# A two-layer pair-attention kernel: in layer 0, both attends of a period are put beside scores, and queries and keys are projected row by row

## What is computed

```python
x = group_norm(x); x = (x - mu) * rsqrt(var + EPS) * ln_w + ln_b
q, k, v = proj(wq), proj(wk), proj(wv)
g = sigmoid(proj(wg_w) + wg_b)
bias = einsum('hc,bcij->bhij', wb, x)
scores = einsum('bhcij,bhcik->bhijk', q, k) * scale + bias[:, :, None, :, :]
a = softmax(scores, axis=-1)
o = g * einsum('bhijk,bhcik->bhcij', a, v)
x = x + einsum('oc,bcij->boij', wrep_w, o) + wrep_b
```

## Time and profile before

| | |
|---|---|
| median of 3 runs | 4764.48 us (4764.19 to 4767.61) |
| the profiled execution | 4769.83 us |
| its span, first to last instruction | 4768.0 us |
| TensorE busy with matmuls | 4524.0 us (95%) |
| DVE, ACT, POOL busy | 3883.6, 3755.4, 3632.2 us |
| layer 0, first to last `residual` | 492.2 to 2785.2 us |

### The profile page before, as it was taken

The page is one execution under the profiler, slowest core; times in us unless marked ns, Lnnn a source line. Parts: engine busy times, 40 slices in busy tenths (PEclk is TensorE's granted clock), DMA queues, the critical chain, the costliest instruction groups (busy, mean ns, idle before and its releaser), DMA issues. The chain is left out here.

```text
span 4768.0 us, 152284 instructions
## 1 busy us (share of the span) xinstructions
PE 4524.0 (95%) x43063; PEld 3665.8 (77%) x43063; DVE 3883.6 (81%) x12844; ACT 3755.4 (79%) x11408; POOL 3632.2 (76%) x6054
## 2 busy tenths in 40 slices
PE   5556999999999999999999979999999999999998
PEld 1224777777777777777777768888888998888887
DVE  5443888889888888888888968888888888888887
ACT  2335888888888888888888868888888888888886
POOL 3442888888888889888888837777777777777776
PEclk7778999999999999999999989999999999999999
DMA  9996111111111111111111111111111111111111
GB/s 359 353 352 196 55 63 53 62 62 53 62 53 62 53 62 58 56 61 54 62 53 62 54 36 55 53 53 53 53 53 53 49 50 53 53 53 53 53 53 35
DMA packets 237444, 383.57 MB, mean 80 GB/s; under 512 B 18756, under 2 KB 156616, under 8 KB 224968
## 3 DMA queue, kind: packets, MB, share of 16 engines
q1 hardware_dynamic: 237256, 381.63, 23.7%
HBM read 309.21 MB, written 72.35 MB: 80 GB/s over the span
## 5 line engine op out<-in xcount | busy, mean ns | idle before, releaser
L1758 POOL TENSOR_SCALAR l_probs<-l_probs,l_inv 128x256 f32<-128x256 f32 x2048 | 947.8, 482 | 374.0 <-DVE l_inv L1655 374.0
L713 POOL TENSOR_SCALAR l_probs<-l_probs,l_inv 128x256 f32<-128x256 f32 x2048 | 944.0, 482 | 118.4 <-DVE l_inv L1140 117.9
L1040 ACT ACTIVATE l_probs<-l_probs,l_neg_max 128x256 f32<-128x256 f32 x2048 | 1019.3, 501 | 12.0 <-DVE l_neg_max L1132 4.4
L1556 ACT ACTIVATE l_probs<-bank,l_neg_max 128x256 f32<-128x256 f32 x2048 | 944.8, 477 | 46.0 <-DVE l_neg_max L1649 39.2
L1662 DVE TENSOR_TENSOR l_probs_t<-bank,bias 128x512 f32<-128x512 f32 x1024 | 669.8, 686 | 130.5 <-PE bank L1468 116.2
L1132 DVE CUSTOM_DVE_ANT_0 l_probs<-bank,bias 128x256 f32<-128x256 f32 x2048 | 744.0, 420 | 25.2 <-issue 12.9
L1649 DVE TENSOR_REDUCE l_neg_max<-bank 128x2 f32<-128x512 f32 x1024 | 675.2, 682 | 43.0 <-PE bank L1456 33.9
L931 PE MATMUL bank<-ident,l_probs 128*128 128x128 f32 x4096 | 615.1, 278 | 0.3 <-ACT l_probs_t L1079 0.3
L931 PEld LDWEIGHTS bank<-ident,l_probs 128*128 128x128 f32 x4096 | 467.9, 141 | 137.6 <-issue 44.3
L1468 PE MATMUL bank<-ident,l_probs 128*128 128x128 f32 x4096 | 559.9, 274 | 5.3 <-POOL l_probs L1758 3.9
L969 PE MATMUL bank<-l_probs_t,l_v 128*64 128x256 f32 x4096 | 498.5, 385 | 0.7 <-ACT l_probs_t L1079 0.7
(11 more groups left out here) (205 smaller groups left out, 13617.6 us busy)
## 6 DMA issues: line engine op xcount, KB each, us to landing
fp_x<-in_x_dram SPq DMA_DIRECT2D x32, 1024.0 KB, 6.2
fp_ln_w<-in_L_conv_ln_w_dram SPq DMA_DIRECT2D x32, 1024.0 KB, 8.3
fp_ln_b<-in_L_conv_ln_b_dram SPq DMA_DIRECT2D x32, 1024.0 KB, 10.8
fp_pair<-in_L_conv_pair_repr_dram SPq DMA_DIRECT2D x32, 1024.0 KB, 10.8
l_x<-in_x_dram SPq DMA_DIRECT2D x128, 256.0 KB, 2.9
l_ln_w<-in_L_conv_ln_w_dram SPq DMA_DIRECT2D x128, 256.0 KB, 3.2
l_ln_b<-in_L_conv_ln_b_dram SPq DMA_DIRECT2D x128, 256.0 KB, 3.5
x<-l_y SPq DMA_DIRECT2D x128, 256.0 KB, 2.0
```

The costliest lines, as they stand in the source:

```text
L713: last = nc.gpsimd.tensor_scalar(probs[:, r, h, c], probs[:, r, h, c], inv[:, r, h, c:c + 1], 1.0, ALU.mult, ALU.mult)
L1040: last = nc.scalar.activation(probs[:, r, h, c], probs[:, r, h, c], ACT.Exp, bias=neg_max[:, r, h, c:c + 1], scale=-1.0, accum_out=total[: ...
L1556: last = nc.scalar.activation(probs[:, h, c], b_s[h % 4][:, c * W:(c + 1) * W], ACT.Exp, bias=neg_max[:, h, c:c + 1], accum_out=total[:, h ...
L1758: last = nc.gpsimd.tensor_scalar(probs[:, h, c], probs[:, h, c], inv[:, h, c:c + 1], 1.0, ALU.mult, ALU.mult)
```

## The change

In words:

- Queries and keys are projected for one row at a time, both halves of the channels into one bank: six matmuls of 256 columns a call, 24 a pair, where there were 12 of 512. The tiles `q` and `k` hold a pair once, by rows, not twice.
- The orders of all engines are new. On TensorE both attends stand directly ahead of the scores of a row (attend of row 1, then scores of row 0; attend of row 0 at the end of the period, then scores of row 1 at the start of the next). Normalising and the first projections run four pairs ahead, not three.
- The banks change: `attend` of row 0 goes to bank 1 and of row 1 to bank 0, `values` of row 0 to bank 0. The waits change with them.
- `join` is spread over two loop bodies, two instructions a call; twice as many bodies of DVE's program stand outside the loop.

The diff, cut to its core (the tables of turns follow the orders and are left out; so are those of POOL):

```diff
-        body(t, False, False)
+        if done < stop:
+            with hinted.Fori(done, stop, engines=[engine.engine], hint_back_edge=True) as t:
+                body(t, False, False)
...
-    AHEAD = 3
+    AHEAD = 4
-    R_BANK = {("AV", 0): 0, ("AV", 1): 1, ("G", 0): 0, ("G", 1): 0, ("K", 0): 1, ("K", 1): 0, "OUT": 0, ("Q", 0): 1, ("Q", 1): 1, ("V", 0): 1, ("V", 1): 1}
+    R_BANK = {("AV", 0): 1, ("AV", 1): 0, ("G", 0): 0, ("G", 1): 0, ("K", 0): 1, ("K", 1): 0, "OUT": 0, ("Q", 0): 1, ("Q", 1): 1, ("V", 0): 0, ("V", 1): 1}
-        q = sb_pair("q", [P, 2, HC, ROWS, W])
-        kk_ = sb_pair("k", [P, 2, HC, ROWS, W])
+        q = sb_pair("q", [P, ROWS, HC, W])
+        kk_ = sb_pair("k", [P, ROWS, HC, W])
...
-                both_rows(b_r[bank], [w[:, 0, j] for w in m.wqk], k).then_inc(q_mm, 1)
+                for j in range(HC):
+                    last = matmul_split(nc, b_r[bank][:, j * W:(j + 1) * W], [w[:, 0, j] for w in m.wqk], [x_[:, k % 2, r] for x_ in xn])
+                last.then_inc(q_mm, 1)
...   keys, row 1
                     bank = 0
-                    if exists(p - 1):
-                        pe.wait_ge(g_ready, GATES_OUT.count(p - 1, 0))
+                    if exists(p):
+                        pe.wait_ge(g_ready, GATES_OUT.count(p, 0))
...   attend, row 0
-                    bank = 0
+                    bank = 1
                     if exists(p + 2):
                         pe.wait_ge(v_ready, VALUES_OUT.count(p, 0))
-                        pe.wait_ge(k_ready, KEYS_LOW.count(p + 2, 1))
+                        pe.wait_ge(k_ready, KEYS_LOW.count(p + 2, 0))
...   attend, row 1
-                    bank = 1
-                    if exists(p + 2):
-                        pe.wait_ge(v_ready, VALUES_OUT.count(p + 2, 0))
+                    bank = 0
+                    if exists(p + 1):
+                        pe.wait_ge(v_ready, VALUES_OUT.count(p, 1))
+                        pe.wait_ge(g_ready, GATES_OUT.count(p + 1, 1))
...   the join on DVE
-                if isinstance(t, int) and t - 1 in JOINED:
...
-                    for g in range(GROUPS * k + GROUPS // ROWS * r, GROUPS * k + GROUPS // ROWS * (r + 1)):
+                for later in range(2):
+                    if isinstance(t, int) and t - 1 - later in JOINED:
...
+                        mine = GROUPS // ROWS // 2
+                        for g in range(GROUPS * (k % UNROLL) + mine * (2 * r + later), GROUPS * (k % UNROLL) + mine * (2 * r + later + 1)):
...
-            pairs(dve, pair, hinted=nc, stops=[last + 1 for last in JOINED])
+            pairs(dve, pair, hinted=nc, stops=[last + after for last in JOINED for after in (1, 2)])
```

More of the change, by code:

```diff
@@ L606, in layer0 @@
[L606 to L619, removed]
@@ new lines, in keys, with values @@
+                for j in range(HC):
+                    last = matmul_split(nc, b_r[bank][:, j * W:(j + 1) * W], [w[:, 1, j] for w in m.wqk], [x_[:, k % 2, r] for x_ in xn])
+                last.then_inc(k_mm, 1)
+            def values(t, k, r):
+                p = UNROLL * t + k
+                pe.wait_ge(xn_step, NORMALISED.count(p, (r, 5)))
+                if r == 0:
+                    bank = 0
+                    if exists(p - 1):
+                        pe.wait_ge(k_ready, KEYS_LOW.count(p - 1, 1))
+                    elif exists(p - 3):
+                        pe.wait_ge(y_ready, p - 2)
+                    elif exists(p - 2):
+                        pe.wait_ge(g_ready, GATES_OUT.count(p - 2, 1))
@@ L1030, in pair @@
                     scores(t, k + 2, 1, 1)
+                if has(1):
+                    transposes(t, k + 1, 1, 3)
+                if has(3):
+                    values(t, k + 3, 0)
+                if has(2):
+                    values(t, k + 2, 1)
+                if has(1):
+                    transposes(t, k + 1, 1, 2)
+                if has(2):
+                    gates(t, k + 2, 1)
+                if has(3):
+                    queries(t, k + 3, 1)
+                if has(1):
+                    attend(t, k + 1, 1)
+                if has(3):
+                    scores(t, k + 3, 0, 0)
+                    scores(t, k + 3, 0, 1)
+                if has(2):
+                    transposes(t, k + 2, 0, 1)
+                if has(4):
+                    queries(t, k + 4, 0)
+                if has(1):
+                    project_out(t, k + 1)
+                if has(2):
+                    transposes(t, k + 2, 0, 2)
+                    transposes(t, k + 2, 0, 3)
+                if has(4):
+                    keys(t, k + 4, 0)
+                if has(3):
+                    gates(t, k + 3, 0)
+                if has(2):
+                    transposes(t, k + 2, 0, 0)
+                    transposes(t, k + 2, 1, 1)
+                if has(3):
+                    keys(t, k + 3, 1)
+                if has(2):
+                    transposes(t, k + 2, 1, 0)
+                    attend(t, k + 2, 0)
             pairs(pe, pair)
@@ new lines, in pair @@
+                if has(4):
+                    queries_high(t, k + 4, 0)
+                if has(2):
+                    exponents(t, k + 2, 1, 0)
+                    exponents(t, k + 2, 1, 3)
+                    transposed_out(t, k + 2, 0, 2)
+                if has(4):
+                    keys_high(t, k + 4, 0)
+                if has(3):
+                    gates_out(t, k + 3, 0)
+                if has(2):
+                    transposed_out(t, k + 2, 0, 0)
+                if has(3):
+                    exponents(t, k + 3, 0, 1)
@@ L1234, in pair @@
                 if has(2):
[L1235 to L1249 removed]
+                    keys_low(t, k + 2, 1)
                 if has(0):
@@ L1252, in pair @@
                     join(t, k, 0)
-                if has(3):
-                    keys_low(t, k + 3, 0)
-                    keys_low(t, k + 3, 1)
+                if has(1):
+                    transposed_out(t, k + 1, 1, 1)
+                    gated(t, k + 1, 0)
+                if has(2):
+                    biased(t, k + 2, 1, 3)
+                    biased(t, k + 2, 1, 0)
+                if has(1):
+                    transposed_out(t, k + 1, 1, 3)
+                    output_low(t, k + 1, 0)
+                if has(2):
+                    inverse(t, k + 2, 0, 3)
+                    inverse(t, k + 2, 0, 1)
+                    biased(t, k + 2, 1, 1)
+                    biased(t, k + 2, 1, 2)
                 if has(0):
```

384 lines of the change are left out of this document (164 added, 220 removed).

## The result

The changed kernel takes 4858.35 us (median of 6 runs, 4855.34 to 4864.62), against 4764.77 us before: a ratio of 1.0197, with a 95% interval of 1.0186 to 1.0207. It is slower by 94 us. The forecast was 4782 us, with a range to 4804: the direction was right, the size was not.

A forecast was written before the change was run, and what follows sets the result against it. TensorE's own sequence was taken to bound layer 0. A calm period of 17.88 + 0.13 + 0.16 = 18.17 us, 0.22 more over 125 pairs, costs 27.5 us; less 10 for joins, this gave 4782 us, range 4746 to 4804.

The forecast's parts named there:

- ACT, DVE and POOL have the same instructions of the same sizes: Layer 0, engines other than TensorE: their instructions stay as before; no time was added for this.
- TensorE's own sum, 17.88: TensorE's steps over one calm period of layer 0 add up to 17.88 us, against 17.95 before.
- The loss by the split, 0.12: Queries and keys on TensorE: 24 matmuls of 0.12 us instead of 12 of 0.229 lose 0.12 us a period.
- The gain of the adjacency, 0.15: TensorE's order: attend straight to scores makes six tiling mode changes a period instead of seven, gaining 0.15 us.
- The two waits, 0.13 and 0.16: TensorE waits for the gates' tanh to free bank 0: attend of row 1 0.13 us late, keys of row 1 0.16.
- The rest hides.: TensorE's other waits (output, transposes and scores of row 1, queries) add nothing, but have little cover.
- Rival 3: A third wait of TensorE adds 0.15 us a period, giving 4801 us; a large one 0.3, 4820. Chance 0.15.
- Joins, 10 us gained: DVE's joins: 12 us gained in its idle time, 2 lost to stalls outside the loop; net 10, bounds 2 and 20.
- Filling and emptying, nothing: Start and end of the layer's pipeline: no change taken, with 4 us either way.
- rival 1: No wait binds: TensorE keeps its 17.88 us period, 9 us gained and 10 of the joins, 4746 us. Chance 0.20.

The follow-up runs named there:

- with the hint: The changed kernel with the branch hint, which DVE's loops already have, at the back edge of ACT's loop in layer 0: 4792.24 us, ratio 1.0051 to the kernel before.
- the two without the stall: The changed kernel with a branch hint on ACT's layer 0 loop (4792.24 us), or with 100 wait and no-operation pairs ahead of that loop (4793.14 us).
- the run with the short gate: The changed kernel with the hint on ACT's loop and the gate's tanh on 32 of 256 columns of each row: 4734.7 us, ratio 0.9929.
- the runs with whole joins: The changed kernel with the hint on ACT's loop and the join as before, four instructions a call in one body: 4805.19 us, ratio 1.0075.

## Why the prediction was wrong, point by point

**What failed.** The step is "ACT, DVE and POOL have the same instructions of the same sizes", and under it the rule that a new order costs only what its steps and waits cost. The sum held stalls in code for DVE's joins alone. It had no term for ACT's loop, whose code is six instructions longer (296 and not 290; the trace has 295 and 289 records from branch to branch) and, behind a longer lead of four pairs, ends at instruction 997 of ACT's program in place of 935. There ACT stands idle for 2.6 to 3.1 us at each of 29 back edges, and layer 0 is 70 us longer for it. Its length is not what matters: the 290 of the kernel before stall where they end at 1000, and the 296 do not where they end at 1097. The rest, 4792 with the stall away, is inside the forecast's own range, partly by luck, as the books below show. The Trainium skill ("Runtime: NRT & Kernel Launch", Instruction fetch mechanics) says that the instruction buffer holds two blocks of 256 instructions and that a taken branch to a block outside of it stalls. The trace agrees that the time goes at the branch (3.5 us to the next instruction); with the two blocks it agrees in part only, as told below. The prediction read that rule for DVE's straight code only, where it would have had to ask it of every loop. The places of ACT's loops of 273 to 296 instructions, counted in the programs and not shown by the profile: those that end at 935, 1097, 1730, 1738 and 1838 show no stall, those that end at 997, 1000 and 1795 do.

**The terms in order.**
- *TensorE's own sum, 17.88.* Measured 17.80 where no bank is late. The loss by the split, 0.12, came from a step read as 0.12 and is 0.02 at most (1.59 against 1.57 for keys, nothing for queries). With 0.117 the sum is 17.82. The gain of the adjacency, 0.15, fits this, but no run measured it alone.
- *The two waits, 0.13 and 0.16.* Both are there and both were priced low; they cost 0.23 and 0.24. The place of the error is the restart: I took 0.05 us from ACT's end to TensorE from one case; at these two steps it is 0.145. An idle TensorE is not the reason: the gates behind ACT's stall start 0.05 after the copy that they wait for, after 1.26 us of idle time, 29 times. What decides between the two distances is not shown. The period came out at 18.28, for 18.17.
- *"The rest hides."* Right: with the hint, the only wait of TensorE that the view lists in the calm stretch of 540 us is the attend's (the keys' wait is hidden in the modelled end of the transposes). Rival 3 did not come.
- *Joins, 10 us gained.* Right by itself: 9 us. In the new order 21 us came back, the far end of the bounds (20, all is hidden).
- *Filling and emptying, nothing.* The first residual came 7.6 us earlier in the run of the changed kernel, 1.3 to 3.4 earlier in the two without the stall. Within the 4 us for these two. Of the 7.6, 3.9 were there at the first projection of queries already (436.6 for 440.5), behind a first part whose code did not change.

**The books.** With the hint, 23 us more than before from first to last residual: 124 periods at 18.28 for 17.94 are 42 more, the last three 2 more, and joins and odd stalls 21 less. The forecast had 27.5 and 10 for these: the calm periods cost 15 us more than it said and the joins gave back 11 more, so that two errors nearly cancel. The stall at ACT's back edge adds 70. In all 93. Of rival 1 (no wait binds) the mechanism is refuted, since the waits bind; its period, 17.88, is near the 17.80 of the run with the short gate.

**What stays open.** The exact rule by which a loop's place gives a stall. The page's two blocks fit the 1795 (its loop begins at 1523, so it touches three), while 997 and 1000 end some 25 short of a block's border counted from the program's first instruction. A constant shift of the count cannot be the reason: one large enough to put 997 over its border would put the loop from 1523 to 1795 into two blocks. That the next block is fetched early and takes the place of the first fits all eight places (those without a stall end 54 or more short of a border), but no run tests it. The stalls of DVE in code outside its loops, which in the kernel before cost some 1 to 3 us at each place with a join, were not explained further.

## What to carry to other kernels

When an order written for several engines is changed, each engine's loop moves in its program, and a back edge can start to cost 3 us each time round: look for idle time with no releaser at the head of a loop, once per run through it, before blaming the order, and test it by a hint or by moving the code with instructions that run once. A loop that has the hint is not safe from it, as DVE's second loop showed. When a matmul stage takes over a PSUM bank soon after another, count from the last matmul: end, ACT's start, the whole read-out, and up to 0.15 us until TensorE starts; here two such waits of 0.23 us turned a better order into a worse one. A time that fits an expectation proves nothing about its cause until the trace shows the time in the expected place, as the runs with whole joins and with the split of queries and keys showed.

## What the runs showed of the hardware

- A satisfied wait and a no-operation, 65 times, run once, made a kernel 49 us slower (ratio 1.0105), 46 of it through the place of two loops.
- The hint at the back edge of a loop of 296 instructions brought the time from the branch to the next instruction from 3.5 us to 0.21. On DVE, loops with the hint still had 3.1 to 3.4 us there in one run (five times) and 1.75 in another (four times).
- Matmuls of 256 columns are 0.117 us apart and of 512 columns 0.229: halving the columns and doubling the number, in 12 matmuls a period, changed nothing that could be measured (ratio 1.0003, 0.9994 to 1.0013).
- From the end of an ACT instruction to the start of the matmul that waits for it: 0.145 us at the attend and at keys (119 times each), 0.05 at the gates behind ACT's stall (29 times), TensorE being idle in all of them.
